# A fused recurrence and feed-forward layer on one core: two absolute sums, a scale and a split moved between three engines in the set-up

## The chip, the cores and the metric

The kernel runs on one core of a Trainium2 chip. The metric is the device time of one execution in microseconds. The core has five engines with queues of their own: TensorE (PE, with its weight loads as PEld), VectorE (DVE), ScalarE (ACT), GpSimd (POOL) and SyncE (SP, which here only issues DMAs). They meet only through semaphores.

## The reference, cut to what matters

```
x: (8, 2048, 256)                                   # 16384 tokens, 256 wide
r = sigmoid(x @ Wr); k = x @ Wk; v = x @ Wv
state = cumsum(k * v / scale) * scale               # scale = decay ** t
y = rmsnorm(r * state) * ln_w
x1 = layernorm(x + y @ Wo)
bw1 = mean|w1| * sign(w1), bw2 = mean|w2| * sign(w2)    # per row of w1 (1024x256) and of w2 (256x1024)
h = gelu(x1 @ bw1.T + b1)
out = layernorm(x1 + h @ bw2.T + b2)
```

The means of w1's and w2's absolute values are `alpha1` and `alpha2` in the kernel. Products in float32 quality are made of two float16 parts: a high part (the scaled value rounded) and a low part (what the rounding lost).

## The kernel before, in words

The tokens are 32 chunks of 512. One chunk passes the three projections (`R`, L375), the scan (`scans`), the output product (`O`, L401 and L406), the first layer norm (`residual1`, `ustats`, `norm1`), the first feed-forward product (`F1`, L446, eight tiles of 512 columns called hc 0 to 7), the gelus (`gelu`, L678), the split into `hid_hi` (`hh`, L713, ScalarE) and `hid_lo` (`hl`, L1008, VectorE), the second product (`F2`, L496) and the second norm. Three chunks are under way at once. Each engine has its instructions written out by hand, first a set-up (`prologue`) and then `step`, once for each chunk; nothing but this order and the semaphores decides what runs when.

The change lies in the set-up's last third, where the constants of the feed-forward part are made while chunks 0 to 2 go through for the first time. The stations there are:

- `alphas2` (ScalarE, L773) sums |w2| in two instructions with 1024 columns each. Before, both stand behind `r_gates(2, 2, (0,))` and ahead of `x1h(0, 1)`.
- `x1h(0, 1)` (ScalarE, L673) takes the high part of chunk 0's x1 out of PSUM, where TensorE's transposes `T1` (L336) put it. `x1l(0)` (VectorE, L992) takes the low part, the one that the change's title calls the residual's. `F1` needs both.
- `hidden_bound` (VectorE, L1160 to L1164) makes from `alpha1` a bound on the hidden values. TensorE spreads its maximum over the partitions with `sum_wmax` (L480). Behind that stand, in TensorE's order, `sum_bounds(1)` (L474) and the first `F1` tiles. `take_bounds` (L896) reads the result of `sum_bounds(1)`, and `hidden_scale` (L1168 to L1171) that of `sum_wmax`; it makes `hid_scale`.
- `alpha2` is multiplied by the bound in one small VectorE instruction at the end of `hidden_scale` (L1173). GpSimd then builds the diagonal matrices `diag` (`diagonal`, L1316), which TensorE turns into a row of `alpha2` (L531), needed when `F2`'s result is scaled.
- `root_rms` (GpSimd, L1322 and L1325) makes the factor `rms` that `residual1` waits for; `root_u` (GpSimd, L1331 to L1338) makes `u_rstd`, which `norm1(1, 0, 1)` (VectorE, L977) waits for.
- `hl(0, pairs[n], first=True)` makes `hid_lo` of two tiles of chunk 0 at a time. Before `hl(0, pairs[1])` stands `norm1(1, 0, 1)` in VectorE's order. `F2(0)` waits for each pair.

Of the kernel before, what the change touches and what calls it, by code (L numbers as in the profile page):

```python
# [27 lines left out]
def postln_layer_kernel(nc, x, Wr, Wk, Wv, Wo, decay, ln_w, w1, b1, w2, b2, out):  # L28
# [4 lines left out]
    H = w1.shape[0]  # L33
# [4 lines left out]
    DC = D // P  # L38
    HC = H // P
# [14 lines left out]
    with ctx:  # L54
# [165 lines left out]
        s_diag, s_arow = sem("diag_s"), sem("arow_s")  # L220
        s_hidden, s_hread, s_row = sem("hidden_s"), sem("hidden_read_s"), sem("alpha2_row_s")
        s_xsq, s_xroot = sem("xsq_s"), sem("xroot_s")
        s_zst, s_zmv, s_zve, s_zrstd, s_zout = sem("zst_s"), sem("zmv_s"), sem("zve_s"), sem("zrstd_s"), sem("zout_s")
        s_zlast = sem("zlast_s")
        s_uneg, s_ushift = sem("uneg_s"), sem("ushift_s")
        s_zneg, s_zshift = sem("zneg_s"), sem("zshift_s")
# [408 lines left out]
        def _(act):  # L635
# [73 lines left out]

            def hh(c, part):  # L710

                act.wait_ge(s_gelu, HC * c + part.stop)
                nc.scalar.activation(hid_hi[:, part, :], hid[:, part, :], ACT.Copy,  # L713
                                     scale=hid_scale[:, :]).then_inc(s_hh, part.stop - part.start)

# [52 lines left out]

            def alphas2():

                act.wait_ge(s_w2_in, 16)
                for dc in range(DC):
                    nc.scalar.activation(w2_in[:, dc, :], w2_in[:, dc, :], ACT.Abs,  # L773
                                         accum_out=alpha2[:, dc:dc + 1]).then_inc(s_alpha, 1)
# [7 lines left out]
            def prologue():  # L782
# [29 lines left out]
                r_gates(2, 2, (0,))  # L812
                act.wait_ge(s_sgn2, 1)
                alphas2()
                x1h(0, 1)
                ysq(1, (1,), y=y_second)
                r_gates(2, 2, (1,))
                act.wait_ge(s_ready, 1)
                gelu(0, range(0, 1))
# [60 lines left out]
        def _(dve):  # L880
# [285 lines left out]
            def hidden_scale():  # L1166
# [109 lines left out]
        def _(pool):  # L1276
# [127 lines left out]
            def prologue():  # L1404
# [75 lines left out]
```

## Time and profile before

| what | value |
| --- | --- |
| time, median of 3 runs | 821.07 us (820.94 to 821.75) |
| time of the profiled execution | 821.11 us |
| its span, first to last instruction | 819.3 us |
| TensorE busy / VectorE busy | 798.8 us (97%) / 771.3 us (94%) |
| ScalarE busy / GpSimd busy | 679.9 us (83%) / 295.3 us (36%) |
| mean granted TensorE clock | 0.998 of full speed |

The profiled execution took 0.04 us more than the median, and 1.8 us of it lie outside of the span. A busy share is a mean over the whole span; the change touches only the stretch from about 40 to 68 us.

### The profile page before, as it was taken

Reading aid. Unit: us, or ns where it says so; the run is one execution under the profiler, and the core shown is the slowest. Engines: PE = TensorE matmul, PEld = TensorE weight load, DVE = VectorE, ACT = ScalarE, POOL = GpSimd, SP = SyncE. Lnnn points to the kernel's source line nnn. Section 1 sums busy time; section 2 is a strip of 40 time slices with the busy share of each in tenths; the row PEclk is TensorE's granted clock in tenths of the full one; section 3 lists DMA queues with packets and bytes.
Section 4 is the critical chain, followed back from the end, with each engine's and each line's share of the span. In section 5 each row is a group of like instructions: output and inputs, shape, how many; then the busy total and the mean of one; then the engine's idle time right before and its main releaser. Section 6 shows DMA issues by size and latency. Waiting matters only on the chain.

```text
span 819.3 us, 16575 instructions
## 1 busy us (share of the span) xinstructions
PE 798.8 (97%) x5174; PEld 505.7 (62%) x5174; DVE 771.3 (94%) x1472; ACT 679.9 (83%) x973; POOL 295.3 (36%) x572
## 2 busy tenths in 40 slices
PE   6989999999999999999999999999999999999986
PEld 4555666656666656666656666655666665666654
DVE  7998999999999999999999999999999999999887
ACT  7987888888888888888888888888888888887775
POOL 3343323344223344333344333344333334332344
PEclk9999999999999999999999999999999999999999
DMA  8513553434553434553434454444454344444313
GB/s 261 99 27 78 129 125 84 110 94 102 128 128 86 115 81 105 125 128 92 113 79 109 118 128 100 105 89 106 112 128 105 100 97 104 106 102 104 78 26 104
DMA packets 168286, 86.27 MB, mean 105 GB/s; under 512 B 128572, under 2 KB 163912, under 8 KB 168264
## 3 DMA queue, kind: packets, MB, share of 16 engines
q1 hardware_dynamic: 147288, 52.97, 27.5%
q0 software_dynamic: 4608, 16.78, 10.4%
q10 hardware_dynamic: 16368, 16.25, 5.6%
q8 instruction: 11, 0.18, 0.1%
q14 instruction: 11, 0.09, 0.0%
HBM read 20.45 MB, written 16.78 MB: 45 GB/s over the span
## 4 chain that ended last, share of the span: by engine, by line
PE 88%; DVE 4%; POOL 2%; ACT 2%; issue 2%; DMA 0%; SPq 0%; POOLq 0%; DVEq 0%; ACTq 0%
PE ps_r L375 28%; PE ps_o L496 26%; PE ps_f L446 19%; PE ps_r L446 6%; PE ps_o L401 6%; PE ps_o L406 3%; DVE hid_lo L1008 1%; DVE u L959 1%; ACT hid L678 1%; DVE u_st L967 0%; PE ps_s L383 0%; DMA x_in<-in_L_attn_x_dram 0%; POOL root L1322 0%; POOL y_sqs L1310 0%; DVE state L923 0%
## 5 line engine op out<-in xcount | busy, mean ns | idle before, releaser
L496 PE MATMUL ps_o<-w2T,hid_hi 128*128 128x256 f16 x992 | 218.9, 273 | 3.4 <-DVE hid_lo L1008 3.0
L496 PE MATMUL ps_o<-w2T,hid_lo 128*128 128x256 f16 x992 | 218.8, 272 | 0.0
L375 PE MATMUL ps_r<-x_t,proj_hi 128*128 128x512 f16 x768 | 197.1, 379 | 1.2 <-issue 0.7
L446 PE MATMUL ps_f<-x_t,w1T 128*128 128x512 f16 x768 | 181.7, 379 | 1.6 <-DVE x_t L992 1.3
L678 ACT ACTIVATE hid<-ps_f,rows_c,f_scale 128x512 f32<-128x512 f32 x192 | 145.2, 774 | 42.2 <-PE ps_f L446 37.1
L1008 DVE SCALAR_TENSOR_TENSOR hid_lo<-hid,hid_scale,hid_hi 128x1024 f16<-128x1024 f32 (+1 forms) x136 | 160.3, 1222 | 0.9 <-POOL hid_hi L1343 0.6
L1310 POOL TENSOR_TENSOR y_sqs<-y_sq 128x512 f32<-128x512 f32 x32 | 46.7, 1459 | 309.6 <-ACT y_sq L653 309.6
L375 PEld LDWEIGHTS ps_r<-x_t,proj_hi 128*128 128x128 f16 x768 | 74.7, 98 | 91.3 <-issue 2.8
L713 ACT ACTIVATE hid_hi<-hid,hid_scale 128x2048 f16<-128x2048 f32 (+2 forms) x72 | 127.9, 1778 | 3.2
L446 PEld LDWEIGHTS ps_f<-x_t,w1T 128*128 128x128 f16 x768 | 74.9, 98 | 79.7 <-issue 1.6
L375 PE MATMUL ps_r<-x_t,proj_lo 128*128 128x512 f16 x384 | 114.2, 379 | 0.2 <-DVE proj_lo L1084 0.2
L496 PEld LDWEIGHTS ps_o<-w2T,hid_hi 128*128 128x128 f16 x992 | 97.0, 98 | 20.2 <-DVE hid_lo L1008 5.9
L496 PEld LDWEIGHTS ps_o<-w2T,hid_lo 128*128 128x128 f16 x992 | 97.1, 98 | 14.4
L647 ACT ACTIVATE r_tanh<-ps_r,x_scl 128x512 f32<-128x512 f32 x64 | 43.9, 686 | 32.6 <-PE ps_r L375 29.4
L653 ACT ACTIVATE y_sq<-y 128x512 f32<-128x512 f32 x62 | 39.1, 630 | 37.0 <-ACT res L707 15.9
L446 PE MATMUL ps_r<-x_t,w1T 128*128 128x512 f16 x256 | 69.6, 378 | 0.0
L707 ACT ACTIVATE res<-res,z_shift,z_rstd 128x256 f32<-128x256 f32 x126 | 65.1, 589 | 4.8 <-POOL z_shift L1356 2.6
L1322 POOL TENSOR_TENSOR root<-ms,neg_half 128x4 f32<-128x4 f32 x32 | 32.8, 1024 | 93.0 <-DVE ms L949 93.0
L375 PEld LDWEIGHTS ps_r<-x_t,proj_lo 128*128 128x128 f16 x384 | 37.5, 98 | 45.7 <-DVE proj_lo L1084 0.9
L696 ACT ACTIVATE res<-u,u_shift,u_rstd 128x256 f32<-128x256 f32 x120 | 61.9, 588 | 1.7 <-POOL u_shift L1338 1.7
L923 DVE TENSOR_TENSOR_SCAN state<-decay_f,state,kvg 128x512 f32<-128x512 f32 x48 | 61.5, 1281 | 0.8
L401 PE MATMUL ps_o<-wo_lo,y_hi 128*128 128x256 f16 x248 | 59.2, 272 | 0.0
(191 smaller groups left out, 1332.2 us busy)
## 6 DMA issues: line engine op xcount, KB each, us to landing
x_in<-in_L_attn_x_dram SPq DMA_DIRECT2D x32, 512.0 KB, 4.1
res<-b_row POOLq DMA_DIRECT2D x32, 512.0 KB, 4.5
out_dram<-res ACTq DMA_DIRECT2D x31, 512.0 KB, 2.9
w_in<-in_L_ffn_w_dram SPq DMA_DIRECT2D x2, 1024.0 KB, 8.8
x_t<-x_st SPq DMA_TRANSPOSE x59, 3.7
b_row<-in_L_ffn_b_dram SPq DMA_DIRECT2D x1, 512.0 KB, 12.7
proj_in<-in_L_attn_Wk_dram SPq DMA_DIRECT2D x1, 256.0 KB, 3.8
proj_in<-in_L_attn_Wv_dram SPq DMA_DIRECT2D x1, 256.0 KB, 4.1
```

The costliest lines, as they stand in the source:

```text
L375: last = nc.tensor.matmul(ps_r[:, m, :], w[:, m, dc, ec * P:(ec + 1) * P], xx[:, :, dc, :], start=(n == 0), stop=(n == 3 * DC - 1))
L401: nc.tensor.matmul(dst[:, tt, :], y_hi[:, dc, tt * P:(tt + 1) * P], w[:, dc, :], start=(dc == 0 and n == 0), stop=False)
L446: last = nc.tensor.matmul(f1_bank[hc % NF], w1T[:, hc, dc, :], xx[:, :, dc, :], start=(dc == 0 and n == 0), stop=(dc == DC - 1 and n == 1))
L496: last = nc.tensor.matmul(o_tok[:, tt, :], hh[:, hc, tt * P:(tt + 1) * P], w2T[:, :, hc, :], start=(hc == 0 and n == 0), stop=(hc == HC - ...
L647: nc.scalar.activation(r_tanh[:, ec, :], ps_r[:, 2, :], ACT.Tanh, scale=x_scl[:, j, 4:5]).then_inc(s_r, 1)
L678: nc.scalar.activation(hid[:, hc, :], f1_bank[hc % NF], ACT.Gelu, bias=b1c[:, hc:hc + 1], scale=f1_scale[:, hc:hc + 1]).then_inc(s_gelu, 1)
L696: nc.scalar.activation(res[j][:, tt, :], u[:, tt, :], ACT.Identity, bias=u_shift[:, tt:tt + 1], scale=u_rstd[:, tt:tt + 1]).then_inc(s_x1, 1)
L707: nc.scalar.activation(res[j][:, tt, :], res[j][:, tt, :], ACT.Identity, bias=z_shift[:, tt:tt + 1], scale=z_rstd[:, tt:tt + 1]).then_inc( ...
L713: nc.scalar.activation(hid_hi[:, part, :], hid[:, part, :], ACT.Copy, scale=hid_scale[:, :]).then_inc(s_hh, part.stop - part.start)
L923: nc.vector.tensor_tensor_scan(state[j % 2][:, ec, :], decay_f[:, ec, :], kvg[:, ec, :], first, ALU.mult, ALU.add).then_inc(s_scan, 1)
L1008: nc.vector.scalar_tensor_tensor(out=hid_lo[:, part, :], in0=hid[:, part, :], scalar=hid_scale[:, :], in1=hid_hi[:, part, :], op0=ALU.mult ...
L1310: nc.gpsimd.tensor_tensor(y_sqs[:, :], y_sq[:, 0, :], y_sq[:, 1, :], ALU.add).then_inc(s_ysqs, 1)
```

## The change

Five edits, all in the set-up. On ScalarE, the two sums of `alphas2` move: the first behind `r_gates(2, 2, (1,))`, ahead of the first gelu, and the second between the gelus of hc 2 and hc 3. The high part of `pairs[1]` (tiles 2 and 3) of chunk 0 leaves ScalarE and becomes one GpSimd instruction (`hh_first`). The product of `alpha2` with the bound leaves VectorE and stands on GpSimd ahead of `diagonal`. GpSimd's order becomes `scales`, `root_rms`, `unscales`, `hh_first`, `diagonal`, `root_u`, `x1b`. On VectorE, `x1l(0)` moves ahead of `hidden_bound()`. ScalarE's next `hh` counts two tiles more on its semaphore, so that later counts stay what they were.

```diff
@@ ScalarE
-            def alphas2():
+            def alphas2(dcs):
                 act.wait_ge(s_w2_in, 16)
-                for dc in range(DC):
+                act.wait_ge(s_sgn2, 1)
+                for dc in dcs:
                     nc.scalar.activation(w2_in[:, dc, :], w2_in[:, dc, :], ACT.Abs,
                                          accum_out=alpha2[:, dc:dc + 1]).then_inc(s_alpha, 1)
...
                 r_gates(2, 2, (0,))
-                act.wait_ge(s_sgn2, 1)
-                alphas2()
                 x1h(0, 1)
                 ysq(1, (1,), y=y_second)
                 r_gates(2, 2, (1,))
+                alphas2((0,))
                 act.wait_ge(s_ready, 1)
                 gelu(0, range(0, 1))
                 yh(1, y_second)
                 gelu(0, range(1, 2))
                 act.wait_ge(s_ready, 2)
                 hh(0, pairs[0])
-                gelu(0, range(2, 4))
-                hh(0, pairs[1])
-                gelu(0, range(4, 6))
-                hh(0, pairs[2])
+                gelu(0, range(2, 3))
+                alphas2((1,))
+                gelu(0, range(3, 6))
+                hh(0, pairs[2], counted=2)
                 gelu(0, range(6, 8))
@@ VectorE
-                if first:
+                if first and part.start == 2:
+                    dve.wait_ge(s_hh_pool, 1)
+                elif first:
                     dve.wait_ge(s_hh, part.stop)
...
                 nc.vector.tensor_scalar_mul(hid_scale[:, :], w_scl[:, 5:6], HTOP).then_inc(s_ready, 1)
-                dve.wait_ge(s_alpha, HC + DC)
-                nc.vector.tensor_scalar(alpha2[:, :], alpha2[:, :], w_max[:, 5:6], 1.0 / (H * HTOP), ALU.mult,
-                                        ALU.mult).then_inc(s_hidden, 1)
...
                 scans(1, 1, 1, y_second)
+                x1l(0)
                 hidden_bound()
-                x1l(0)
                 take_bounds(1, 3)
                 hidden_scale()
@@ GpSimd
+            def hh_first(part):
+
+                pool.wait_ge(s_gelu, part.stop)
+                pool.wait_ge(s_ready, 2)
+                nc.gpsimd.tensor_scalar(hid_hi[:, part, :], hid[:, part, :], hid_scale[:, :], 1.0, ALU.mult,
+                                        ALU.mult).then_inc(s_hh_pool, 1)
+
             def diagonal():
 
-                pool.wait_ge(s_hidden, 1)
+                pool.wait_ge(s_alpha, HC + DC)
+                pool.wait_ge(s_hread, 1)
+                nc.gpsimd.tensor_scalar(alpha2[:, :], alpha2[:, :], w_max[:, 5:6], 1.0 / (H * HTOP), ALU.mult,
+                                        ALU.mult).then_inc(s_alpha2, 1)
+                pool.wait_ge(s_alpha2, 1)
...
                 scales(3, 3)
-                diagonal()
                 root_rms(1)
                 unscales(3, 3)
+                hh_first(pairs[1])
+                diagonal()
+                root_u(1, True)
                 pool.wait_ge(s_b2_in, 16)
                 x1b(0, 0)
-                root_u(1, True)
```

VectorE's order around the bound, before the change. The first row is the last instruction of `scans` on chunk 1 (it writes y into x1's staging tile, shown as `x_st`), the four rows behind it are `hidden_bound`, `x_t` is `x1l(0)`, the next three are `take_bounds`, three are `hidden_scale` with `alpha` behind them, and `state` begins the scan of chunk 2.

```order
L926 SCALAR_TENSOR_TENSOR x_st<-r_tanh,state 128x512 [waits scan_s]
L1160 SCALAR_TENSOR_TENSOR hid_bound<-rows_c 128x8 [waits rows_s,alpha_s]
L1162 TENSOR_TENSOR hid_bound<-hid_bound,alpha 128x8 [waits dve_setup_chain]
L1163 TENSOR_REDUCE w_max<-hid_bound 128x1 [waits dve_setup_chain]
L1164 TENSOR_SCALAR f_scale<-alpha 128x8
L992 SCALAR_TENSOR_TENSOR x_t<-ps_f,x_t 128x1024 [waits x1h_s]
L896 TENSOR_REDUCE y_q<-ps_s 128x1 [waits bounds_s]
L898 TENSOR_SCALAR x_scl<-ps_s 128x1
L901 TENSOR_SCALAR y_q<-y_q 128x1 [waits yq_s]
L1168 TENSOR_SCALAR w_max<-ps_s 128x1 [waits wsum_s]
L1170 RECIPROCAL w_scl<-w_max 128x1 [waits hidden_read_s]
L1171 TENSOR_SCALAR hid_scale<-w_scl 128x1 [waits dve_setup_chain]
L1173 TENSOR_SCALAR alpha<-alpha,w_max 128x2 [waits alpha_s]
L923 SCALAR_TENSOR_TENSOR state<-decay_f,state,kvg 128x512 [waits r_s,kvg_s]
```

The same place in the changed kernel.

```order
L927 SCALAR_TENSOR_TENSOR x_st<-r_tanh,state 128x512 [waits scan_s]
L993 SCALAR_TENSOR_TENSOR x_t<-ps_f,x_t 128x1024 [waits x1h_s]
L1163 SCALAR_TENSOR_TENSOR hid_bound<-rows_c 128x8 [waits rows_s,alpha_s]
L1165 TENSOR_TENSOR hid_bound<-hid_bound,alpha 128x8 [waits dve_setup_chain]
L1166 TENSOR_REDUCE w_max<-hid_bound 128x1 [waits dve_setup_chain]
L1167 TENSOR_SCALAR f_scale<-alpha 128x8
L897 TENSOR_REDUCE y_q<-ps_s 128x1 [waits bounds_s]
L899 TENSOR_SCALAR x_scl<-ps_s 128x1
L902 TENSOR_SCALAR y_q<-y_q 128x1 [waits yq_s]
L1171 TENSOR_SCALAR w_max<-ps_s 128x1 [waits wsum_s]
L1173 RECIPROCAL w_scl<-w_max 128x1 [waits hidden_read_s]
L1174 TENSOR_SCALAR hid_scale<-w_scl 128x1 [waits dve_setup_chain]
L924 SCALAR_TENSOR_TENSOR state<-decay_f,state,kvg 128x512 [waits r_s,kvg_s]
```

`x1l(0)` has moved from behind the four rows of `hidden_bound` to ahead of them, `take_bounds` follows `hidden_bound` directly, and the row of `alpha` is gone.

GpSimd's order at the end of its set-up, before the change, from `scales(3, 3)` on.

```order
L1280 TENSOR_TENSOR x_scl<-x_scl,neg_half 128x1 [waits xtmp_s]
L1316 TENSOR_SCALAR diag<-ident,alpha 128x128 [waits hidden_s]
L1316 TENSOR_SCALAR diag<-ident,alpha 128x128
L1322 TENSOR_TENSOR root<-ms,neg_half 128x4 [waits ms_s]
L1325 TENSOR_TENSOR rms<-root,y_inv 128x4 [waits yinv2_s,root_s]
L1285 TENSOR_TENSOR x_root<-x_scl 128x1 [waits xscl_s]
L1287 TENSOR_TENSOR x_scl<-w_inv,x_root 128x3 [waits xroot_s]
L1295 DMA res<-b_row 128x1024 [waits zadd_s,b2_in_s,x1l_s]
L1331 TENSOR_SCALAR u_ve<-u_mv 128x4 [waits umv_s]
L1333 TENSOR_TENSOR u_rstd<-u_ve,neg_half 128x4 [waits uve_s]
L1335 TENSOR_SCALAR u_neg<-u_mv 128x4
```

The same place in the changed kernel.

```order
L1280 TENSOR_TENSOR x_scl<-x_scl,neg_half 128x1 [waits xtmp_s]
L1333 TENSOR_TENSOR root<-ms,neg_half 128x4 [waits ms_s]
L1336 TENSOR_TENSOR rms<-root,y_inv 128x4 [waits yinv2_s,root_s]
L1285 TENSOR_TENSOR x_root<-x_scl 128x1 [waits xscl_s]
L1287 TENSOR_TENSOR x_scl<-w_inv,x_root 128x3 [waits xroot_s]
L1316 TENSOR_SCALAR hid_hi<-hid,hid_scale 128x1024 [waits weights_ready_s,gelu_s]
L1323 TENSOR_SCALAR alpha<-alpha,w_max 128x2 [waits hidden_read_s,alpha_s]
L1327 TENSOR_SCALAR diag<-ident,alpha 128x128 [waits alpha2_s]
L1327 TENSOR_SCALAR diag<-ident,alpha 128x128
L1342 TENSOR_SCALAR u_ve<-u_mv 128x4 [waits umv_s]
L1344 TENSOR_TENSOR u_rstd<-u_ve,neg_half 128x4 [waits uve_s]
```

The rows of `diag` have moved from ahead of `root` to behind the new rows of `hid_hi` and `alpha`, and all four now stand ahead of `u_ve` and `u_rstd`, where no instruction but the DMA stood.

## Rows read from the trace of the kernel before

**Rows 1.** The page: busy time, share of the span, instructions.

```profile
PE 798.8 (97%) x5174; PEld 505.7 (62%) x5174; DVE 771.3 (94%) x1472; ACT 679.9 (83%) x973; POOL 295.3 (36%) x572
```

**Rows 2.** Windows: length, busy us of PE, PEld, DVE, ACT, POOL, clock, DMA.

```profile
68.00:800.00 732.00, 729.82 (x4752) 462.94 (x4751) 698.84 (x1314) 614.29 (x862) 262.31 (x505) 1.00 0.43 104
...
814.00:816.00 2.00, 0.00 (x0) 0.00 (x0) 0.78 (x4) 1.09 (x2) 0.89 (x3) 1.00 0.24 83
```

**Rows 3.** Timeline of PE, 42 to 64 us: start, duration, [idle before <-releaser].

```profile
42.05 1.04 PE L336 MATMUL ps_f<-ident,res 128*128 128x128 f32 x8
...
44.80 0.18 PE L474 MATMUL ps_s<-bounds,ones 128*128 128x3 bf16 x1 [0.42 <-ACT y_sq L653]
45.55 1.89 PE L446 MATMUL ps_f<-x_t,w1T 128*128 128x512 f16 x8 [0.56 <-DVE x_t L992]
...
48.94 0.37 PE L383 MATMUL ps_s<-y_part,fold 128*128 128x16 f32 x2 [0.65 <-DVE y_part L939]
...
51.78 1.89 PE L446 MATMUL ps_f<-x_t,w1T 128*128 128x512 f16 x8
...
63.14 0.28 PE L496 MATMUL ps_o<-w2T,hid_hi 128*128 128x256 f16 x1 [1.29 <-DVE hid_lo L1008]
```

**Rows 4.** Timeline of VectorE, 43 to 58 us.

```profile
43.42 0.16 DVE L1160 SCALAR_TENSOR_TENSOR hid_bound<-rows_c 128x8 f32<-128x8 f32 x1
...
43.81 0.16 DVE L1163 TENSOR_REDUCE w_max<-hid_bound 128x1 f32<-128x8 f32 x1
...
44.17 1.23 DVE L992 SCALAR_TENSOR_TENSOR x_t<-ps_f,x_t 128x1024 f16<-128x1024 f32 x1
45.32 0.15 DVE L896 TENSOR_REDUCE y_q<-ps_s 128x1 f32<-128x2 f32 x1
...
46.02 0.24 DVE L1173 TENSOR_SCALAR alpha<-alpha,w_max 128x2 f32<-128x2 f32 x1
46.17 1.27 DVE L923 TENSOR_TENSOR_SCAN state<-decay_f,state,kvg 128x512 f32<-128x512 f32 x1
...
48.09 0.70 DVE L939 TRANSPOSE_TENSOR_REDUCE y_part<-y_sqs 128x16 f32<-128x512 f32 x1
...
50.08 0.17 DVE L949 TENSOR_REDUCE ms<-ms_all 128x4 f32<-128x16 f32 x1
50.52 1.28 DVE L1008 SCALAR_TENSOR_TENSOR hid_lo<-hid,hid_scale,hid_hi 128x1024 f16<-128x1024 f32 x1 [0.27 <-ACT hid_hi L713]
51.90 1.66 DVE L959 SCALAR_TENSOR_TENSOR u<-ps_o,rms,x_in 128x256 f32<-128x256 f32 x4
...
56.15 0.75 DVE L914 SCALAR_TENSOR_TENSOR kvg<-ps_r,x_scl,k_sb 128x512 f32<-128x512 f32 x1
56.96 1.40 DVE L977 TENSOR_SCALAR res<-u,u_mv,u_rstd 128x256 f32<-128x256 f32 x4
```

**Rows 5.** Timeline of ScalarE, 42 to 54 us.

```profile
42.69 0.19 ACT L773 ACTIVATION_READ_ACCUMULATOR w_in<-w_in 128x1 f32 x1
43.12 1.02 ACT L673 ACTIVATE x_t<-ps_f 128x1024 f16<-128x1024 f32 x1 [0.24 <-PE ps_f L336]
...
46.67 0.78 ACT L678 ACTIVATE hid<-ps_f,rows_c,f_scale 128x512 f32<-128x512 f32 x1 [1.34 <-PE ps_f L446]
...
52.84 0.78 ACT L678 ACTIVATE hid<-ps_f,rows_c,f_scale 128x512 f32<-128x512 f32 x1 [1.76 <-PE ps_f L446]
```

**Rows 6.** Timeline of GpSimd, 48 to 57 us.

```profile
48.04 0.73 POOL L1316 TENSOR_SCALAR diag<-ident,alpha 128x128 f32<-128x128 f32 x2
...
51.44 0.43 POOL L1325 TENSOR_TENSOR rms<-root,y_inv 128x4 f32<-128x4 f32 x1
...
55.63 0.19 POOL L1331 TENSOR_SCALAR u_ve<-u_mv 128x4 f32<-128x4 f32 x1 [1.79 <-DVE u_mv L971]
55.90 1.03 POOL L1333 TENSOR_TENSOR u_rstd<-u_ve,neg_half 128x4 f32<-128x4 f32 x1
```

**Rows 7.** GpSimd's splits of 512 columns in the last chunks: duration ns min/median/max.

```profile
L1343 POOL TENSOR_SCALAR hid_hi<-hid,hid_scale x6: 687/778/1196, 784.5 to 806.4; 128x512 f16<-128x512 f32 x6
```

More of the change, by code:

```diff
@@ L220, in postln_layer_kernel @@
         s_diag, s_arow = sem("diag_s"), sem("arow_s")
-        s_hidden, s_hread, s_row = sem("hidden_s"), sem("hidden_read_s"), sem("alpha2_row_s")
+        s_hread, s_row = sem("hidden_read_s"), sem("alpha2_row_s")
         s_xsq, s_xroot = sem("xsq_s"), sem("xroot_s")
@@ L224, in postln_layer_kernel @@
         s_zlast = sem("zlast_s")
+        s_alpha2, s_hh_pool = sem("alpha2_s"), sem("hh_pool_s")
         s_uneg, s_ushift = sem("uneg_s"), sem("ushift_s")
@@ L708, in norm2, with hh @@
                                          bias=z_shift[:, tt:tt + 1], scale=z_rstd[:, tt:tt + 1]).then_inc(s_zout, 1)
-            def hh(c, part):
+            def hh(c, part, counted=0):
                 act.wait_ge(s_gelu, HC * c + part.stop)
                 nc.scalar.activation(hid_hi[:, part, :], hid[:, part, :], ACT.Copy,
-                                     scale=hid_scale[:, :]).then_inc(s_hh, part.stop - part.start)
+                                     scale=hid_scale[:, :]).then_inc(s_hh, part.stop - part.start + counted)
             act.wait_ge(s_rows, 1)
```

## The prediction, as put on record before the changed kernel ran

> **What bounds the kernel now.** The page comes first, for the shares: TensorE is busy 97% of the span and VectorE 94% [rows 1]. That is a mean, and the change touches only the set-up, so the windows come next: from 68 to 800 us TensorE is busy 729.8 of 732 us [rows 2]. The body runs without pauses. So a delay or a gain in the set-up that moves the end of TensorE's first `F2` passes to the end of the kernel one for one, and one that moves only another engine is swallowed.
>
> The third view is TensorE's timeline from 42 us on, read for its pauses [rows 3]. It waits 0.42 us for ScalarE's y_sq, 0.56 us for VectorE's `x1l(0)`, 0.65 us for VectorE's y_part, and 1.29 us for the last pair's `hid_lo`. Behind that last pause (end 63.14) it never stops again. Nearly all of these pauses name VectorE, so the fourth view is VectorE's timeline [rows 4]: it is packed from 43 to 63 us, and its longest marked idle stretch is 0.27 us, before the first `hid_lo`. VectorE sets the end of this stretch. Its only partners on the path are the engines that it waits for: ScalarE's `x1h` at 44.17, and GpSimd's `rms` and `u_rstd` [rows 6].
>
> **The change, part by part.** I follow the instants in the new order, each with the durations of the rows of before.
>
> *ScalarE's sums.* The two sums end at 42.88 (42.69 + 0.19), and `x1h` starts at 43.12, released by TensorE's transposes, which end at 43.09 (42.05 + 1.04) [rows 3, 5]. Taking the sums away widens a wait that TensorE ends: `x1h` stays at 43.12 and ends at 44.14. Gain 0. In their new places they cost nothing either. One takes about 1.03 us; ScalarE is idle for 1.34 us ahead of the gelu at 46.67 and for 1.76 us ahead of the one at 52.84 [rows 5], and both gelus will be later, not sooner (below). If that cover were gone, each would cost at most its 1.03 us.
>
> *`x1l(0)` sooner.* It starts at 44.17 before, and ScalarE's `x1h` ends at 44.14 [rows 4, 5]. So VectorE had filled its wait for `x1h` with `hidden_bound` (from 43.42 on). Now it idles there, `x1l` starts at 44.17 again, and `hidden_bound` follows at 45.32 in place of 43.42. Its maximum is ready 0.39 + 0.16 us later (43.81 - 43.42 is 0.39), at 45.87. TensorE's `sum_wmax` waits for it, and `sum_bounds(1)` and `F1` are queued behind it. With 0.15 us from VectorE to TensorE (45.40 to 45.55, and 48.79 to 48.94 [rows 3, 4]), `sum_wmax` runs at 46.02, `sum_bounds` at 46.05 with 0.18 us, and `F1` at about 46.08, 0.53 us late. VectorE's `take_bounds` waits for `sum_bounds`: 46.23 plus 0.07 for the way back (an estimate; TensorE to ScalarE took 0.03 at 43.12) is 46.30, where it was 45.32. From there to the scan it took 0.85 us, of which 0.15 us (46.02 to 46.17) were the `alpha` row that is gone: 0.70. The scan of chunk 2 starts at 47.00, **0.83 us late**.
>
> *What follows the scan.* y_part ends at 49.62 in place of 48.79, `O` starts at 49.77, and the `F1` tile behind it at 52.61 (51.78 + 0.83). The gelu of hc 3 starts 1.06 us after that, at 53.67, and ends at 54.45. The first high part on ScalarE shifts with `F1`, by 0.53 us; it released VectorE's first `hid_lo` at 50.52 after a wait of 0.27 us [rows 4], and now does at 51.05. VectorE was free at 50.25 and, 0.83 us late, is free at 51.08, so this wait is gone. But the mean of squares `ms` is 0.83 us late (50.91), and `root` and `rms` with it. Before, `rms` ended at 51.87 and u started at 51.90; now `rms` ends at 52.47 if it takes 0.20 us, and 52.70 if again 0.43 us. u is thus 0.6 to 0.83 us late; I take 0.7. `norm1` would follow kvg at 56.82 + 0.7 = 57.52 (56.15 + 0.75 less the overlap of 0.08; before it waited until 56.96 for `u_rstd`, which ended at 56.93).
>
> *GpSimd's new work.* `hh_first` waits for the gelu of hc 3 and starts at 54.52. The trace has no such instruction of 1024 columns. From below it can't be under that of 512 columns, 0.69 us; from above it is twice the longest of those, 2.39 us [rows 7]. Two `diag` of 128 columns take 0.73 us, 0.37 each [rows 6], so 384 columns more cost 0.32 us, and 512 more 0.42 to 0.43. I take 0.69 + 0.42, and round to 1.15 us: VectorE then runs statistics of u, which read one tensor. It ends at 55.67. `alpha2`'s product is nearly empty, 0.2 us like `rms`' shortest kind, then 0.08 us for the wait on itself: 55.97. `diag` 0.73: 56.70. `root_u` has its input since about 56.3 (55.63 [rows 6] + 0.7), but runs only now; from `u_ve` to `u_rstd` it takes 0.27 us: 57.03 with 0.06 us for its waits. With 1.03 us `u_rstd` ends at 58.06, and `norm1` starts at **58.09, 1.13 us late**, behind a wait of 0.57 us. Queued behind it on VectorE are `hl(pairs[1])`, `hl(pairs[2])`, `x1l_rows` and `hl(pairs[3])`, for which `F2(0)` waits. Nothing fills that gap.
>
> A rule of the Trainium skill (GPSIMD Engine Reference, section 3.1) bears on `hh_first`: an elementwise body with few operations is bound at 1.03 cycles an element, while a loop unrolled by four reached 1.8 cycles, 769 ns for 512 elements. The rows' 0.32 us for 384 columns go with the first. By the second, 1024 columns would be an estimated 1.54 us, and the sum 0.4 us larger. Section 4.1 of the page advises VectorE for such work; the rule speaks against this edit.
>
> *What is saved.* ScalarE's high part of pair 1 (1.15 us) was not waited for: VectorE comes to it only behind `norm1`, at 58.3 (56.96 + 1.40). Without it the gelu of hc 4 follows sooner and `F1`'s last tile may start sooner, but `F2` waits for VectorE anyway. Worth 0.
>
> **Sum.** +0.83 from the bound, -0.13 regained ahead of u, +0.57 for GpSimd less the 0.14 us that `norm1` waited already: 1.13. From `norm1` on, before's durations hold: TensorE's last pause ends at 64.27 and not at 63.14. On the profiled execution's 821.11 us this gives 822.24; its time is 0.04 us over the median, so I say **822.2 us**, 0.14% more. A measurement of this kernel tells about 0.2% (1.64 us) from no change, so this counts as no change.
>
> **The rivals.**
> - *Only VectorE's delay counts.* If `hh_first` takes 0.7 us, `norm1` is bound by VectorE at 57.5 and not by GpSimd: +0.6 to +0.7, 821.7 us. It decides below about 0.6 us of `hh_first`, just off the lower bound.
> - *GpSimd is far later (slower).* Its instruction is drawn out as in the longest rows: 2.0 to 2.39 us for `hh_first`, or 0.43 for small ones. Then `norm1` starts 0.9 to 1.25 us later still: +2.0 to +2.4, 823.4 us. From 1.66 us of `hh_first` on the kernel is slower by over 0.2%. For it: the last chunks' rows reach 1196 ns while VectorE makes `hid_lo`. Against: VectorE makes statistics at 54.5. The Trainium skill (GPSIMD Engine Reference, section 8) says that GpSimd's SBUF interfaces suffer from VectorE instructions with two SBUF inputs.
> - *The clock falls.* TensorE gets pauses of 1.6 us (44.4 to 46.0) and about 1.9 us (59.1 to 61). If the granted clock fell to 1.2 GHz, several us of products would take twice as long: 824 to 825 us. Against: it is still 1.00 in 814 to 816, in which TensorE ran nothing [rows 2].
> - *Faster.* All four waits in front of `F2`'s pairs would have to shrink. If `x1h` came as soon as ScalarE is free, by up to 2.3 us, VectorE's chain would start sooner and the time be 819 to 820 us. It needs the transposes' end before 41.4, and they start at 42.05.
> - *It does nothing:* the bound's way through TensorE is cheaper than worked out and GpSimd just in time: 820.7 to 821.3.
>
> **How the numbers follow.** The forecast (821.9 to 822.7) has 0.52; only VectorE's delay 0.14; no effect 0.08; GpSimd far later 0.16; the clock 0.03; faster 0.07. The range takes 0.1 off either end: 821.1 to 823.4. Slower by over 0.2% (above 822.7) is GpSimd far later, the clock and the upper edge of the forecast, 0.27; faster by over 0.2% (below 819.4) is 0.07; the rest, 0.66, is the same.
>
> **What would show it.** In the profile of the changed kernel: `x1h` at 43.12 and `x1l` at 44.17 as before; `w_max` at 45.7 and TensorE's L474 at 46.05, with a pause of over 1.5 us ahead of it; an idle stretch of VectorE ahead of y_q; the scan at 47.0; GpSimd's `hid_hi` from 54.5, 1.15 us long; `norm1` released by GpSimd's `u_rstd` at about 58.1; TensorE's last pause ending at 64.3. The prediction is wrong if `x1h` starts before 43, if `hid_hi` takes over 1.6 us, or if pauses appear behind 68 us.

## The result and the profile after

The changed kernel takes 825.13 us (median of 6 runs, 824.33 to 826.45), the kernel before beside it 821.07 us (6 runs, 820.94 to 821.75). The ratio is 1.005, with a 95% interval of 1.0037 to 1.0063: 4.1 us slower. The prediction was 822.2 us, no change that can be measured; the time lies above its range. The profiled execution of the changed kernel took 826.45 us with a span of 824.7 us and a granted clock of 0.995; that of before had a span of 819.3 us. So 5.4 us are to be found, in the slowest of the six runs. Three of them read a mean clock of 0.995 and took 825.70 to 826.45 us, the other three read 0.998 or 0.999 and took 824.33 to 824.57 us; only the first was profiled, so what else sets the two groups apart can't be read.

The page shows almost nothing of them. TensorE is busy for 3.0 us more than in [rows 1], with the same 5174 instructions, so some of them took longer:

```profile
PE 801.8 (97%) x5174; PEld 506.7 (61%) x5174; DVE 771.8 (94%) x1471; ACT 679.1 (82%) x972; POOL 300.3 (36%) x574
```

A list of one instruction at the same place in every chunk (`y_sqs`, GpSimd) finds them: the changed kernel is 1.47 us behind at chunks 0 and 1, 4.01 us at chunk 2 and 4.04 us at chunk 30, and 6.06 us at chunk 31, of which 5.4 are left at the end. The losses have three places: the head, before the change begins (1.47 us), the stretch of the change (2.54 us), and the tail (about 1.4 us, after 2.02 us at chunk 31). The head is not the change's. There a weight matrix came late by DMA in this one execution, as the first row of VectorE's timeline shows; in the same program run again, and in nine other experiments, it did not, and in two (e2 and e6) it was late by less, 0.81 and 0.56 us. All instants of this profile behind it have to be read 1.47 us earlier.

VectorE's timeline of the changed kernel, in the head and at the bound:

```profile
9.86 0.69 DVE L1077 TENSOR_REDUCE w_max<-proj_in 128x1 f32<-128x512 f32 x1 [1.14 <-DMA proj_in<-in_L_attn_Wv_dram]
...
45.65 1.23 DVE L993 SCALAR_TENSOR_TENSOR x_t<-ps_f,x_t 128x1024 f16<-128x1024 f32 x1 [0.67 <-ACT x_t L674]
46.79 0.80 DVE L1163 SCALAR_TENSOR_TENSOR hid_bound<-rows_c 128x8 f32<-128x8 f32 x1
...
47.83 0.16 DVE L1166 TENSOR_REDUCE w_max<-hid_bound 128x1 f32<-128x8 f32 x1
...
48.46 0.16 DVE L897 TENSOR_REDUCE y_q<-ps_s 128x1 f32<-128x2 f32 x1 [0.39 <-PE ps_s L475]
...
49.18 1.29 DVE L924 TENSOR_TENSOR_SCAN state<-decay_f,state,kvg 128x512 f32<-128x512 f32 x1
```

These rows answer to [rows 4]. Take off 1.47 us: `x1l` starts at 44.18 against 44.17, behind an unfilled wait, as worked out; it is 0.67 us long. But the first row of `hidden_bound`, 8 columns, takes 0.80 us in place of 0.16, and the scan starts at 47.71: 1.54 us late, not 0.83. What GpSimd does at that time is in its timeline:

```profile
46.30 1.26 POOL L1310 TENSOR_TENSOR y_sqs<-y_sq 128x512 f32<-128x512 f32 x1 [4.66 <-ACT y_sq L654]
...
57.37 1.12 POOL L1316 TENSOR_SCALAR hid_hi<-hid,hid_scale 128x1024 f16<-128x1024 f32 x1 [1.94 <-ACT hid L679]
58.48 0.26 POOL L1323 TENSOR_SCALAR alpha<-alpha,w_max 128x2 f32<-128x2 f32 x1
58.83 0.72 POOL L1327 TENSOR_SCALAR diag<-ident,alpha 128x128 f32<-128x128 f32 x2
```

`y_sqs` runs from 46.30 to 47.56, and `hid_bound` ends at 47.59. The small instruction did not take long; it could not end before the large one of the other engine had. Further down, `hid_hi` takes 1.12 us where 1.15 us was forecast, and `alpha` and `diag` 0.26 and 0.72 us.

TensorE's timeline of the changed kernel, which answers to [rows 3]:

```profile
48.13 0.16 PE L481 MATMUL ps_s<-w_max,ones 128*128 128x1 bf16 x1 [2.28 <-DVE w_max L1166]
48.26 0.16 PE L475 MATMUL ps_s<-bounds,ones 128*128 128x3 bf16 x1
48.38 3.04 PE L447 MATMUL ps_f<-x_t,w1T 128*128 128x512 f16 x8
...
67.14 0.28 PE L497 MATMUL ps_o<-w2T,hid_hi 128*128 128x256 f16 x1 [1.28 <-DVE hid_lo L1011]
```

And its windows (length, busy us of PE, PEld, DVE, ACT, POOL, clock, DMA):

```profile
46.00:48.00 2.00, 0.00 (x0) 0.00 (x0) 1.93 (x5) 1.84 (x5) 1.26 (x1) 1.00 0.00 0
...
49.00:52.00 3.00, 3.00 (x8) 1.06 (x7) 2.93 (x6) 2.19 (x3) 1.88 (x3) 0.50 0.03 5
```

The pause ahead of the sum is 2.28 us, not 1.6. Behind it the granted clock is 0.50 (1.2 GHz) for 3 us, and the first eight products of `F1` take 3.04 us where they took 1.89 [rows 3]. TensorE's last pause ends at 67.14, 4.00 us behind [rows 3], or 2.53 us without the head.

The third place is chunk 30, the last but one, at its first norm. GpSimd's rows of the changed kernel there, and the wait that comes of them on VectorE and TensorE:

```profile
768.01 0.19 POOL L1342 TENSOR_SCALAR u_ve<-u_mv 128x4 f32<-128x4 f32 x1 [1.75 <-DVE u_mv L972]
768.29 1.91 POOL L1344 TENSOR_TENSOR u_rstd<-u_ve,neg_half 128x4 f32<-128x4 f32 x1
770.28 0.95 POOL L1346 TENSOR_SCALAR u_neg<-u_mv 128x4 f32<-128x4 f32 x1
771.38 1.05 POOL L1349 TENSOR_TENSOR u_shift<-u_neg,u_rstd 128x4 f32<-128x4 f32 x1 [0.15 <-POOL u_neg L1346]
...
768.05 1.27 DVE L1011 SCALAR_TENSOR_TENSOR hid_lo<-hid,hid_scale,hid_hi 128x1024 f16<-128x1024 f32 x1
...
775.66 1.22 DVE L988 SCALAR_TENSOR_TENSOR x_st<-res,x_st 128x1024 f16<-128x1024 f32 x1 [2.10 <-ACT x_st L670]
...
783.28 0.16 PE L475 MATMUL ps_s<-bounds,ones 128*128 128x2 bf16 x1 [0.52 <-ACT y_sq L654]
```

The same place in before, GpSimd and then VectorE:

```profile
763.65 0.19 POOL L1331 TENSOR_SCALAR u_ve<-u_mv 128x4 f32<-128x4 f32 x1 [1.44 <-DVE u_mv L971]
763.92 1.01 POOL L1333 TENSOR_TENSOR u_rstd<-u_ve,neg_half 128x4 f32<-128x4 f32 x1
...
765.81 0.20 POOL L1338 TENSOR_TENSOR u_shift<-u_neg,u_rstd 128x4 f32<-128x4 f32 x1 [0.48 <-POOL u_neg L1335]
...
764.00 1.27 DVE L1008 SCALAR_TENSOR_TENSOR hid_lo<-hid,hid_scale,hid_hi 128x1024 f16<-128x1024 f32 x1
```

Before, `u_rstd`, `u_neg` and `u_shift` took 1.01, 0.31 and 0.20 us. In the changed kernel `u_rstd` starts 0.24 us behind VectorE's `hid_lo`; before, it started 0.08 us ahead of it (763.92 against 764.00). The place is 700 us from the nearest edit.

### The profile page after: what moved, and what is told of

Same layout as the page of the kernel before. It is cut to its first block, busy times and chain, and to the rows that moved or that the text cites. A ratio compares the mean times of both kernels' runs of the same rounds, so it can differ in the third digit from the quotient of the medians.

```text
span 824.7 us, 16577 instructions
## 1 busy us (share of the span) xinstructions
PE 801.8 (97%) x5174; PEld 506.7 (61%) x5174; DVE 771.8 (94%) x1471; ACT 679.1 (82%) x972; POOL 300.3 (36%) x574
## 4 chain that ended last, share of the span: by engine, by line
PE 85%; DVE 5%; POOL 3%; issue 2%; ACT 2%; DMA 1%; SPq 0%; POOLq 0%; DVEq 0%; ACTq 0%
PE ps_r L376 27%; PE ps_o L497 25%; PE ps_f L447 18%; PE ps_r L447 6%; PE ps_o L402 6%; PE ps_o L407 3%; DVE hid_lo L1011 1%; DMA proj_in<-in_L_attn_Wv_dram 1%; DVE state L924 1%; ACT hid L679 1%; DVE u L960 1%; DVE u_st L968 0%; PE ps_s L384 0%; POOL root L1333 0%; POOL u_rstd L1344 0%
```

## The experiments

Every kernel was run beside the kernel before, whose medians were 821.07 to 821.12 us. The losses are told apart with these readings: what `y_sqs` lags at chunk 2 more than at chunk 0 (the stretch of the change), what it lags at chunk 31 more than at chunk 30 (the tail), and the first `F1` tiles (the clock). The tail's 2.0 us at chunk 31 leave 1.3 to 1.4 at the end.

### The change once more

The same program, with an empty line at its end.

> The changed kernel once more, to see which of its shifts come back. In the first profile TensorE's last set-up pause ended 4.00 us late, made of 1.47 us that were there before 41 us (proj_in landed late) and 2.54 us of the stretch that the change touches; another 1.3 us came in at 767 to 781 us, with slow GpSimd instructions. Theory A (the first and the last shift are chance): they are absent here or have another size, the middle one comes back as 1.8 us without a fall of the clock and 2.5 us with one; the time is 823 to 825 us. Theory B (they belong to the changed program): x1h starts again at 44.6 us and the tail is again 1.3 us late; 825 to 826 us.

It took 824.86 us (5 runs, 824.29 to 824.92; ratio 1.0044, 1.0031 to 1.0058), profiled with a span of 823.0 us. The head is as in before (0.13 us sooner), the stretch of the change costs 2.53 us, and the tail 1.3. VectorE and TensorE of this run:

```profile
45.19 0.80 DVE L1163 SCALAR_TENSOR_TENSOR hid_bound<-rows_c 128x8 f32<-128x8 f32 x1
...
59.36 1.39 DVE L978 TENSOR_SCALAR res<-u,u_mv,u_rstd 128x256 f32<-128x256 f32 x4 [0.54 <-POOL u_rstd L1344]
...
46.54 0.16 PE L481 MATMUL ps_s<-w_max,ones 128*128 128x1 bf16 x1 [2.29 <-DVE w_max L1166]
46.66 0.16 PE L475 MATMUL ps_s<-bounds,ones 128*128 128x3 bf16 x1
46.79 3.41 PE L447 MATMUL ps_f<-x_t,w1T 128*128 128x512 f16 x8
```

So the long `hid_bound`, the pause and the fallen clock come back with the change, and so does the tail's loss, where theory A had expected chance; the late weight matrix does not. `norm1` waits 0.54 us for GpSimd; 0.57 us was forecast.

### The low part alone, and everything but the low part

```diff
@@ before, e2
-                hidden_bound()
                 x1l(0)
+                hidden_bound()
@@ changed kernel, e3
-                x1l(0)
                 hidden_bound()
+                x1l(0)
```

> The kernel before with nothing changed but x1l(0) ahead of hidden_bound(). Theory 1 (the low part's move is the main cost): the wait for x1h is left unfilled, the bound's first instruction waits for GpSimd's y_sqs (0.80 us and not 0.16), and TensorE pauses over 2 us ahead of sum_wmax, so that its clock falls to half in a part of the runs. The scan of chunk 2 starts 1.7 us later than before, and the time is 1.7 us more without a fall and 2.4 us or more with one: 822.8 to 823.8 us. Theory 2 (GpSimd's new work in front of root_u is the main cost): at most 0.7 us more, under 821.9 us.

> The changed kernel with only the low part's move taken back: sums, scale, hh_first and GpSimd's order stay as changed. Theory 1: the scan starts 0.15 us sooner than before, the gelu of hc 3 as before (52.8), hh_first at 53.7, u_rstd ends at 57.3, norm1 is 0.4 us late; 821.2 to 821.7 us, and no fall of the clock. Theory 2: most of the loss stays, over 823 us, with norm1 released by u_rstd about 1 us late or more.

The low part's move alone: 823.40 us (9 runs, ratio 1.0026, 1.0016 to 1.0036), with the stretch 2.45 us longer and no loss in the tail. The change without it: 822.85 us (8 runs, 1.0024, 1.0014 to 1.0035), above the 821.2 to 821.7 us expected, which had left out the tail. The stretch is only 0.23 us longer than before, and about 1.3 us are lost in the tail (0.14 us behind at chunk 30, 2.15 at chunk 31, 1.4 in the span). `hid_bound` takes 0.80 us in the first and 0.16 us in the second. So nearly all that is lost in the set-up comes from one exchange of two calls, and the tail's loss from something in the other four edits. GpSimd's `root` of e2, and VectorE around it:

```profile
52.79 2.07 POOL L1322 TENSOR_TENSOR root<-ms,neg_half 128x4 f32<-128x4 f32 x1 [1.56 <-DVE ms L949]
...
52.69 1.28 DVE L1008 SCALAR_TENSOR_TENSOR hid_lo<-hid,hid_scale,hid_hi 128x1024 f16<-128x1024 f32 x1
55.17 1.27 DVE L959 SCALAR_TENSOR_TENSOR u<-ps_o,rms,x_in 128x256 f32<-128x256 f32 x3 [1.19 <-POOL rms L1325]
```

VectorE's `hid_lo` had begun 0.10 us before it. In before, `root` had its start ahead of `hid_lo` (50.34 against 50.52) and took 1.02 us. `rms` was late by that, and u waited 1.19 us for it. This is a holding up in the other direction: GpSimd waits for VectorE.

So the 2.45 us of e2 are not made up like the 2.53 us of e1. In e2's profiled execution TensorE paused for 2.28 us too, but the clock stayed at 1.00 in each window from 45 to 55 us; in place of the clock's share it has the 1.05 us of `root`. That the two are so near each other is chance.

### Products that bridge the pause

```diff
@@ changed kernel, e4: TensorE, ahead of the sum; nothing reads them
                 pe.wait_ge(s_ms, 1)
+                idle_products(ps_s[:, P:2 * P], 14)
                 sum_wmax(ps_wmax[:, 5:6], 5, 1, 6)
```

> The changed kernel with 14 products whose result nobody reads on TensorE ahead of sum_wmax of the bound, in the pause in which it would stand still. Theory 1 with the clock: the clock stays at full speed in all runs (each at 0.998 or above), the twelve first F1 products take 2.6 us and not 4.3, and the runs near 826 us are gone: the median falls by 0.7 us or more against the changed kernel's, to 824.3 or less. If the clock's fall costs nothing because VectorE is behind anyway: same median as the changed kernel.

824.32 us (5 runs, 824.16 to 826.04; 1.0048, 1.0034 to 1.0062). TensorE and its windows in this run:

```profile
46.46 0.18 PE L481 MATMUL ps_s<-w_max,ones 128*128 128x1 bf16 x1 [0.68 <-DVE w_max L1167]
46.56 0.16 PE L475 MATMUL ps_s<-bounds,ones 128*128 128x3 bf16 x1
46.68 1.89 PE L447 MATMUL ps_f<-x_t,w1T 128*128 128x512 f16 x8
...
49.00:52.00 3.00, 2.17 (x19) 1.53 (x17) 2.87 (x6) 2.89 (x4) 0.61 (x2) 1.00 0.02 5
```

With a pause of 0.68 us the clock stays at 1.00 (2.4 GHz) and the eight products take 1.89 us again. The stretch costs 1.80 us in place of 2.53; by chunk 30 it is 2.05 against 2.56, for a reason that I did not find. The clock's share is 0.5 to 0.7 us, less than the 1.5 us that the products themselves lose, so part of that was covered. By the times alone this gain is not shown, since two of the five runs took 825.8 and 826.0 us. They did so at a mean clock of 0.998, so the expectation that the runs near 826 us would be gone failed, and the clock is not what makes them; what does stays open.

### The tail: filler instructions in before

```diff
@@ before, e5: GpSimd, at the start of its set-up
+                for n in range(4):
+                    nc.gpsimd.memset(fillers[:, n:n + 1], -1.0)
                 scales(1, 1)
...
```

> The kernel before with four tiny memsets added on GpSimd early in its set-up, where it waits over 5 us anyway; nothing else. Theory P (the tail's 1.3 us come from where GpSimd's later code lies, since more instructions stand ahead of it): GpSimd's one short stall of 0.32 us per execution, which before stood ahead of u_shift at 765.8, moves to an earlier instruction; if it falls ahead of u_ve or u_rstd of chunk 30, u_rstd starts behind VectorE's hid_lo and not 0.08 us ahead of it, takes 1.9 us in place of 1.0, and the time is 1.2 to 1.4 us longer: 822.3 us. Theory Q (the tail's loss has to do with the changed work itself): no change, 821.1 us.

822.46 us (11 runs; 1.0016, 1.0007 to 1.0025): 1.4 us lost by four instructions of one column each at 14.6 us. Up to chunk 30 every instant is that of before; chunk 31 is 2.00 us late. GpSimd's rows and VectorE's `hid_lo`:

```profile
763.96 0.19 POOL L1332 TENSOR_SCALAR u_ve<-u_mv 128x4 f32<-128x4 f32 x1 [1.75 <-DVE u_mv L972]
764.24 1.90 POOL L1334 TENSOR_TENSOR u_rstd<-u_ve,neg_half 128x4 f32<-128x4 f32 x1
766.22 0.95 POOL L1336 TENSOR_SCALAR u_neg<-u_mv 128x4 f32<-128x4 f32 x1
767.33 1.05 POOL L1339 TENSOR_TENSOR u_shift<-u_neg,u_rstd 128x4 f32<-128x4 f32 x1 [0.15 <-POOL u_neg L1336]
...
763.99 1.28 DVE L1009 SCALAR_TENSOR_TENSOR hid_lo<-hid,hid_scale,hid_hi 128x1024 f16<-128x1024 f32 x1
```

These are the changed kernel's rows. Once in this stretch GpSimd stands for 0.32 us with nothing in the profile that it waits for. In before this falls ahead of `u_shift`, where nobody minds (its gap is 0.48 us and not 0.15). With four more instructions ahead it falls ahead of `u_ve`, which starts 0.52 us behind the end of `u_mv` and not 0.20. `u_rstd` then misses its start ahead of `hid_lo` by 0.25 us and is held up with the three rows behind it.

### The sums and the scale, and GpSimd's new order

```diff
@@ changed kernel, e6: x1l(0) back, the high part of pairs[1] back on ScalarE, hh_first gone
...
-                hh_first(pairs[1])
                 diagonal()
@@ changed kernel, e7: x1l(0) back, and root_u ahead of diagonal
...
                 hh_first(pairs[1])
-                diagonal()
                 root_u(1, True)
+                diagonal()
@@ e8: as e7, and six fillers as in e5
```

> The changed kernel without the low part's move and without hh_first: the sums sit in ScalarE's breaks, alpha2's scale is on GpSimd, pair 1's high part is back on ScalarE, the diagonals stay behind unscales. If the sums and the scale cost nothing: the set-up ends 0.1 to 0.2 us sooner than before (VectorE has an instruction less), norm1 waits for nothing; 821.0 us, plus 1.3 us if the tail's loss comes with it (one GpSimd instruction more than before).

> The changed kernel with the low part's move taken back and root_u between hh_first and the diagonals. The wait of norm1 for u_rstd (0.30 us in the run with only the low part back) should be gone: u_rstd ends at about 56.8. The set-up then ends as before or 0.1 us sooner, and what is left is the tail's 1.3 us: 822.3 us. If the rest of the loss in that run was not this wait, it stays at 822.5 to 822.9.

> The kernel of e7_root_between with six tiny memsets added on GpSimd early in its set-up. Theory P: the stall moves on by six instructions, off u_ve and u_rstd of chunk 30, into the wait ahead of them or to root_z's instructions; u_rstd takes 1.0 us again and the tail's 1.3 us are gone: 820.9 to 821.2 us. Theory Q: as e7_root_between.

The sums and the scale alone: 821.09 us (11 runs; 1.0000, 0.9991 to 1.0010). They cost nothing and bring nothing. With the high part on GpSimd and `root_u` ahead of `diagonal`: 822.57 us (11 runs; 1.0018, 1.0009 to 1.0027). `norm1` waits for nobody there and starts at 56.75. The stretch costs 0.17 us, hardly less than the 0.23 us of e3, where `norm1` still waits 0.30 us for `u_rstd`: `norm1` and the two `hid_lo` behind it take 1.49 and 2.58 us in e7, where they took 1.40 and 2.47 us before, with GpSimd's `alpha` and `diag` now beside them. Chunk 31 is 2.06 us late again. With six fillers more: 821.29 us (11 runs; 1.0002, 0.9993 to 1.0011), and the tail's loss is gone. The stall now falls ahead of another instruction (`z_ve`, whose wait behind `z_mv` is 1.03 us and not 0.70), and GpSimd's rows of e8 at chunk 30 read:

```profile
763.68 0.19 POOL L1343 TENSOR_SCALAR u_ve<-u_mv 128x4 f32<-128x4 f32 x1 [1.10 <-DVE u_mv L973]
763.95 1.02 POOL L1345 TENSOR_TENSOR u_rstd<-u_ve,neg_half 128x4 f32<-128x4 f32 x1
765.06 0.31 POOL L1347 TENSOR_SCALAR u_neg<-u_mv 128x4 f32<-128x4 f32 x1
```

The fillers were run in both directions, then: four make before slower, six make a version of the change faster. What goes with the loss is where the stall falls.

### The change with six fillers

The edit is that of e8, on the changed kernel itself.

> The changed kernel, all edits in place, with six tiny memsets added on GpSimd early in its set-up. Theory P (where GpSimd's later code lies decides whether u_rstd of chunk 30 loses its place ahead of hid_lo): the tail's 1.3 us are gone and nothing else moves: 823.5 us. If the tail's loss needs GpSimd's old position for another reason: 824.8 us as the changed kernel.

823.69 us (7 runs, 822.99 to 823.96; 1.0031, 1.0020 to 1.0042), profiled at 822.99. The tail's loss is gone; the stretch costs 1.92 us. In this profiled execution the pause of 2.29 us was there and the clock did not fall:

```profile
46.62 0.16 PE L482 MATMUL ps_s<-w_max,ones 128*128 128x1 bf16 x1 [2.29 <-DVE w_max L1167]
46.75 0.16 PE L476 MATMUL ps_s<-bounds,ones 128*128 128x3 bf16 x1
46.87 1.89 PE L448 MATMUL ps_f<-x_t,w1T 128*128 128x512 f16 x8
```

That prices the clock a second time: u starts at 53.23 here and at 53.82 in e1, though the scan stands at 47.67 and 47.59. It is 0.6 to 0.7 us, and the stretch, 1.92 us and not 2.53, says the same. The other six runs of e9 read a mean clock of 0.996 where the profiled one read 0.997, and took 0.6 to 1.0 us more.

### The absolute value ahead of the low part

```diff
@@ changed kernel, e10: hidden_bound's first row, |b1|, taken out of it and moved ahead
+                dve.wait_ge(s_rows, 1)
+                nc.vector.scalar_tensor_tensor(out=hid_bound[:, 0, :], in0=b1c[:, :], scalar=-1.0,
+                                               in1=b1c[:, :], op0=ALU.mult, op1=ALU.max).then_inc(chain, 1)
+                done[0] += 1
                 x1l(0)
+                dve.wait_ge(chain, done[0])
                 hidden_bound()
...
```

> The changed kernel with the first of hidden_bound's instructions, the absolute value of b1, taken ahead of x1l(0); the other three stay behind it. Theory S (VectorE instructions with two SBUF inputs wait while GpSimd's y_sqs runs, until about 45.97): the absolute value takes 0.16 us at 43.3, and the next one, the sum of two small SBUF tiles at 45.2, takes 0.8 us in its place; the time stays within 0.1 us of the changed kernel's 824.8. Theory F (the first small instruction behind x1l is slow whatever it reads, or the absolute value itself is): the 0.64 us are gone with it, TensorE's pause is under 1.7 us, and the time is 0.8 to 1.3 us less.

824.72 us (5 runs; 1.0044, 1.0030 to 1.0058), not told apart from e1 (the stretch costs 2.29 us, the clock is 0.50 from 48 to 50 us, the tail's loss is there). VectorE's rows, and GpSimd's sum:

```profile
43.31 0.16 DVE L1200 SCALAR_TENSOR_TENSOR hid_bound<-rows_c 128x8 f32<-128x8 f32 x1
44.07 1.22 DVE L993 SCALAR_TENSOR_TENSOR x_t<-ps_f,x_t 128x1024 f16<-128x1024 f32 x1 [0.60 <-ACT x_t L674]
45.21 0.80 DVE L1162 TENSOR_TENSOR hid_bound<-hid_bound,alpha 128x8 f32<-128x8 f32 x1
...
44.72 1.26 POOL L1312 TENSOR_TENSOR y_sqs<-y_sq 128x512 f32<-128x512 f32 x1 [4.66 <-ACT y_sq L654]
```

The moved row takes 0.16 us, and the product behind `x1l`, which took 0.17 us in the change, takes 0.80. So it isn't this instruction that is slow; whichever comes first with two operands in SBUF under GpSimd's `y_sqs` (44.72 to 45.98) has to wait for its end. `x1l` began 0.65 us ahead of `y_sqs` and ran beside it until 45.29, and `y_sqs` kept its 1.26 us: `x1l`, of whose two operands one is in PSUM, did not hold it up.

### GpSimd's sum behind the bound

```diff
@@ changed kernel, e11: GpSimd
                 root_u(0)
+                pool.wait_ge(s_wmax, 6)
                 ysqs(1)
```

> The changed kernel with one wait more on GpSimd: y_sqs of chunk 1 starts only when the bound's maximum is made. Theory S: hidden_bound's first instruction takes 0.16 us again, the maximum is ready at 45.75, TensorE's pause shrinks from 2.28 to about 1.7 us, and if that keeps the clock up, the first F1 products take 1.9 us; the scan starts at 46.95 or, if y_sqs then stands in its way, at 47.1. The time is 823.6 to 824.3 us. Theory F: the instruction still takes 0.8 us and the time is 824.8 us or more.

822.94 us (11 runs, 822.73 to 823.48; 1.0021, 1.0012 to 1.0030). TensorE, VectorE and GpSimd of this run:

```profile
45.93 0.16 PE L481 MATMUL ps_s<-w_max,ones 128*128 128x1 bf16 x1 [1.64 <-DVE w_max L1166]
...
45.23 0.16 DVE L1163 SCALAR_TENSOR_TENSOR hid_bound<-rows_c 128x8 f32<-128x8 f32 x1
...
46.98 1.28 DVE L924 TENSOR_TENSOR_SCAN state<-decay_f,state,kvg 128x512 f32<-128x512 f32 x1
...
49.98 1.28 DVE L933 SCALAR_TENSOR_TENSOR y_lo<-x_st,y_roots,y_hi 128x1024 f16<-128x1024 f32 x1 [0.37 <-ACT y_hi L659]
...
47.09 1.67 POOL L1300 TENSOR_TENSOR y_roots<-y_q,halves 128x2 f32<-128x2 f32 x1
```

Here the set-up is what the prediction had worked out: `hid_bound` 0.16 us, a pause of 1.64 us, the scan at 46.98 (forecast: 47.00). The clock is 1.00 in each window from 46 to 52 us, and its mean over the whole span was 0.997 to 0.999 in all 11 runs. But the sum, moved behind the bound, pushes `y_roots` under VectorE's scan, where it takes 1.67 us (0.70 in the change) and ends 0.50 us behind the scan's end. `y_hi` and with it `y_lo` are late, so the stretch still costs 1.75 us. The time came out lower than expected because the tail's loss vanished: `u_rstd` took 1.02 us, and `u_ve` started 0.20 us behind the end of `u_mv`. That the wait added to GpSimd's program had shifted the stall is inferred; no gap in this profile shows where it went.

### All repairs but the order of VectorE

e12 is the changed kernel with the repairs of e4, e8 and e11 together: idle products, `root_u` ahead of `diagonal`, six fillers, and `y_sqs` behind the bound.

> The changed kernel with four repairs: y_sqs behind the bound (e11), 14 idle products ahead of sum_wmax (e4), root_u between hh_first and the diagonals (e7), six memsets (e8). What is left of the change's loss should be the order alone: VectorE's wait for x1h that nothing fills (0.67 us) and the way of the bound through TensorE and back (0.39 us of idle time), less the alpha row of 0.15 us and the waits ahead of u that shrink. That is the 0.83 us of the prediction at the scan, and 0.6 to 0.9 us at the end: 821.7 to 822.0 us. If the repairs don't add up, it is over 822.5 us.

823.40 us (6 runs, 822.74 to 825.23; 1.0030, 1.0017 to 1.0042), above the 821.7 to 822.0 us expected. The expectation failed on the step from the scan on. The scan starts at 46.84, 0.67 us late, but u at 53.28, 1.4 us late: VectorE waits 0.37 us for `y_hi` and 0.43 us for the first `hid_hi`, as in e11. The stretch costs 1.67 us, and the tail nothing. Three of the six runs took 823.88 to 825.23 us and the other three 822.74 to 822.91; what the slower ones lost isn't in the profiled one and stays open. No version was faster than the kernel before.

## Why the prediction was wrong, step by step

- **`x1h` stays, the wait is unfilled.** Right: 44.59 less the head's 1.47 is 43.12, and VectorE idles for 0.67 us.
- **"Its maximum is ready 0.39 + 0.16 us later ..., at 45.87."** This step failed. The 0.39 us holds `hid_bound`'s duration of 0.16 us [rows 4], taken from a place where GpSimd ran nothing, and I moved it under GpSimd's `y_sqs`. It took 0.80 us. The step cost 0.64 us more than I had put, shown by e11 (0.16 us with the sum out of the way) and e10 (the next instruction takes it over). I had looked for this holding up at GpSimd's instructions alone, and `hid_hi`, where I had priced it, did not have it.
- **The round trip of the bound.** Right: from `w_max` through TensorE to `y_q` and to the scan. In e11 the scan starts 0.02 us from the forecast.
- **"u is thus 0.6 to 0.83 us late; I take 0.7."** Held with luck. By the prediction's own instants `root` would start at 51.17 (50.34 in before, and 0.83), 0.09 us behind VectorE's `hid_lo` at 51.08, and e2 shows what 0.10 us behind it costs: 1.05 us. In the changed kernel `hid_hi` and with it `hid_lo` came late enough to leave `root` ahead, by 0.36 us in e1 and by 0.01 us in e9.
- **The clock, a rival with 0.03.** Its argument was a pause of 1.6 us; that pause left the clock at 1.00 (e11). The pause was 2.28 us because of the step before, and behind such a pause the clock fell in some executions (0.50 in the changed kernel and in e1, and behind 2.08 us in e10) and not in others (e2, e9). It costs about 0.5 to 0.7 us (e4, e9 against e1), not the several that I named.
- **GpSimd's new work.** Right in every term: `hid_hi` 1.12 us (forecast 1.15), `alpha` 0.26 (0.2), `diag` 0.72 (0.73), `norm1` released by `u_rstd` behind 0.54 us (0.57). The rival in which GpSimd is far later is refuted. The larger estimate of 1.54 us for `hid_hi` did not come true.
- **The sums, the scale, the high part off ScalarE.** Right: worth nothing (e6, e7).
- **"From `norm1` on, before's durations hold."** This step failed too. The body passes the delay on one for one, as said, but a start missed at chunk 30, which shows at chunk 31, adds about 1.3 us that have nothing to do with the delay. e5 shows that a longer program on GpSimd is enough to cause it. It lay 700 us outside of what I had read.

The sum for e1: 1.13 us as predicted, 0.64 for `hid_bound`, 0.5 to 0.7 for the clock and 1.3 for the tail make 3.6 to 3.8. Its span is 3.7 us longer than that of before. The median of the first six runs is 4.1 us longer; the 0.3 us between it and e1 stay open, and late weights as in the profiled one may be part of them. With the tail and the clock out (e9) the first two make 1.77, and 1.92 was measured. By edits, the low part's move is 2.3 of the 2.5 us in the set-up (e1 less e3). With it taken back, GpSimd's work behind which `root_u` stands costs 0.2, and `root_u` ahead of `diagonal` changes that by 0.06, too little to tell.

What stays open: what the stall of 0.32 us is. Its place depends on the number of instructions ahead of it (e5, e8, e9). A transfer on an instruction queue (`q14` in the DMA view) shifts in the same way: in before it is at 766.6, 0.8 us behind the start of `u_shift`; in the changed kernel, e5, e8 and e9 it is at 768.6, 764.5, 761.2 and 763.1, 0.5 to 0.6 us behind the start of the instruction that came late. In e11 it is at 764.8, while GpSimd waits for `u_mv`, where a stall ahead of the wait would cost nothing. That would fit a load of instruction code; it is argued from the times and not shown. The Trainium skill (Advanced Engine Details and Errata, Sequencer Memory) gives the cores of GpSimd an instruction cache of 16 KB; no run here shows whether the stall has to do with it.

## What to carry to other kernels

When an instruction is moved, its duration is not moved with it: look what the other engine of the pair GpSimd and VectorE runs at the new place. If VectorE's instruction has two operands in SBUF, work out the case in which the one that starts later waits for the other's end. An exchange that fills no wait and empties one is worth looking for first; here it was one pair of calls, and it cost more than all other edits. And before a loss is put down to an edit, compare one instruction chunk by chunk over the whole program: a third of the loss in e1 was a start missed by a quarter of a microsecond, 700 us away, and four fillers in the kernel before bring the same.

## What the runs showed of the hardware that was not expected

- **GpSimd and VectorE hold each other up.** A VectorE instruction with two operands in SBUF takes 0.80 us and not 0.16 if it starts under a GpSimd sum of 1.26 us, and ends with it. The other way round GpSimd's `root` takes 2.07 us and not 1.02 if VectorE's `hid_lo` began 0.10 us sooner, and `u_rstd` 1.91 and not 1.01; both end 0.9 us behind the end of `hid_lo`. `u_neg`, which reads one tensor, is held up too (0.95 us and not 0.31). The exclusion is not of whole instructions: in before `u_rstd` runs from 763.92 to 764.93, and `hid_lo`, which starts at 764.00, takes 1.27 us all the same. The Trainium skill (GPSIMD Engine Reference, section 8) says that there is contention with VectorE instructions that have two SBUF inputs; the trace agrees, with these numbers.
- **A margin of 0.08 us decided over 1.4 us.** In before `u_rstd` starts 0.07 to 0.09 us ahead of `hid_lo` in each chunk from 2 to 30.
- **GpSimd has a stall of 0.32 us** whose place shifts with the number of instructions ahead of it, and a transfer on an instruction queue shifts with it.
- **The clock.** Behind pauses of 2.28 and 2.29 us it was 0.50 in two profiled executions (the changed kernel, e1) and 1.00 in two others (e2, e9); behind one of 1.64 us it stayed at 1.00 (e11), with a mean of 0.997 to 0.999 in all 11 runs of that kernel, as in the kernel before. Which of the two comes behind 2.28 us I can't say from these rows.
